# Turning adj in blocks of 512 rows by 128 columns, out of place

## What is computed

```python
# layer 0: attention with 4 heads, adj as bias and as mask
scores = einsum('hnd,hmd->hnm', qh, kh) * SCALE + graph_bias * adj
scores = where(adj == 0, -1e9, scores);  out = softmax(scores) @ vh ...  @ Wout + bout
# layer 1: graph attention, mask adj > 0 or diagonal
h = softmax(where(mask, leaky_relu(e_src[:, None] + e_dst[None, :]), NEG_INF)) @ (x @ W)
# layers 2 and 3: with d = adj.sum(axis=1) ** -0.5
h = (d[:, None] * adj * d[None, :]) @ x @ W        # then + b, or relu
# after each: x = layernorm(x + h)
```

## Time and profile before

| | us |
|---|---|
| median of 3 runs | 3061.91 |
| lowest and highest | 3058.38, 3064.88 |
| the profiled execution | 3062.02 |
| its span | 3060.1 |

### The profile page before, as it was taken

One profiled execution on the slowest core, in us unless ns is written; L12 is line 12 of the kernel. 1 busy time (PEld: TensorE's weight loads), 2 busy tenths in 40 slices (PEclk: granted clock), 3 DMA queues, 4 the chain that ended last, 5 costly groups with the idle time before them and its releaser, 6 DMA issues.

```text
span 3060.1 us, 45164 instructions
## 1 busy us (share of the span) xinstructions
PE 2959.7 (97%) x16612; PEld 2186.8 (71%) x16612; DVE 2104.1 (69%) x3607; ACT 1885.9 (62%) x2705; POOL 756.0 (25%) x454
## 2 busy tenths in 40 slices
PE   8999999999999999999998899999999999999998
PEld 5677777777777777777776555555558888788887
DVE  6677777777777777777766977777636545565464
ACT  4677777777777777777775677777653333433332
POOL 2123311333113321233210355555501001000000
PEclk9999999999999999999999999999999999999999
DMA  5699998899989998999947243333079988989882
GB/s 184 137 181 193 186 191 175 187 192 207 169 186 190 187 205 178 179 192 195 197 100 278 88 145 137 124 138 138 21 178 212 217 199 201 218 204 218 203 196 59
DMA packets 707435, 534.41 MB, mean 175 GB/s; under 512 B 563728, under 2 KB 603920, under 8 KB 690832
## 3 DMA queue, kind: packets, MB, share of 16 engines
q1 hardware_dynamic: 682176, 445.00, 65.1%
q10 hardware_dynamic: 18144, 66.07, 8.0%
q0 software_dynamic: 6896, 20.45, 2.3%
HBM read 443.29 MB, written 88.08 MB: 174 GB/s over the span
## 4 chain that ended last, share of the span: by engine, by line
PE 68%; DMA 11%; DVE 7%; issue 5%; SPq 4%; POOL 3%; ACT 2%; POOLq 0%; DVEq 0%; ACTq 0%
PE gl_four L1475 12%; PE at_o L606 9%; PE gl_quad L1528 7%; PE gl_quad L1529 7%; PE gl_quad L1530 7%; PE at_turn L580 6%; PE at_turn L593 5%; DMA adjT<-at_probs 4%; PE at_score L580 3%; PE gl_quad L1458 3%; DMA at_probs<-in_adj 3%; PE at_score L593 3%; SPq L404 3%; DMA at_bias<-in_adj 2%; POOL at_masked L503 2%
## 5 line engine op out<-in xcount | busy, mean ns | idle before, releaser
L717 ACT ACTIVATE at_probs<-at_probs,at_minus_max 128x1024 f32<-128x1024 f32 x512 | 581.6, 1139 | 9.6 <-DVE at_minus_max L871 8.7
L866 DVE CUSTOM_DVE_ANT_0 at_probs<-at_turn,at_bias 128x1024 f32<-128x1024 f32 x336 | 407.1, 1212 | 172.4 <-PE at_turn L580 167.3
L503 POOL TENSOR_SCALAR at_masked<-at_bias 128x512 bf16<-128x512 f32 x180 | 365.6, 2043 | 630.9 <-DMA at_bias<-in_adj 624.7
L726 ACT ACTIVATE at_pT<-at_turn 128x1024 f32<-128x1024 f32 x342 | 346.0, 1024 | 252.2 <-PE at_turn L593 251.9
L606 PE MATMUL at_o<-at_pT,at_values 128*64 128x256 f32 x4096 | 470.3, 382 | 0.0
L1475 PE MATMUL gl_four<-gl_early,gl_first_wh 128*128 128x512 f32 x1024 | 460.8, 593 | 6.0 <-ACT gl_early L1596 6.0
L1621 ACT ACTIVATE gl_split<-gl_units 128x1024 fp32r<-128x1024 f32 x256 | 263.7, 1055 | 278.6 <-PE gl_quad L1530 278.6
L580 PE MATMUL at_turn<-at_kT,at_q 128*128 128x512 f32 x1344 | 397.7, 418 | 22.6 <-DVE at_maxima L866 22.6
L1528 PE MATMUL gl_quad<-gl_split,gl_rows_hi 128*128 128x512 f32 x1024 | 403.0, 394 | 6.0 <-DVE gl_split L1809 6.0
L606 PEld LDWEIGHTS at_o<-at_pT,at_values 128*64 128x64 f32 x4096 | 282.5, 137 | 172.8 <-issue 43.2
L1529 PE MATMUL gl_quad<-gl_split,gl_rows_hi 128*128 128x512 f32 x1024 | 399.2, 390 | 0.0
(11 more groups left out here) (135 smaller groups left out, 3880.6 us busy)
## 6 DMA issues: line engine op xcount, KB each, us to landing
gl_units<-adjT SPq DMA_DIRECT2D x512, 256.0 KB, 7.9
at_bias<-in_adj SPq DMA_DIRECT2D x128, 512.0 KB, 6.1
at_probs<-in_adj SPq DMA_DIRECT2D x256, 256.0 KB, 5.4
adjT<-at_probs SPq DMA_DIRECT2D x1024, 64.0 KB, 4.9
gl_first_weights<-in_adj SPq DMA_DIRECT2D x32, 2048.0 KB, 8.2
at_values<-v_heads ACTq DMA_DIRECT2D x126, 512.0 KB, 5.6
gl_early<-x SPq DMA_DIRECT2D x160, 128.0 KB, 2.7
x<-gl_early POOLq DMA_DIRECT2D x64, 128.0 KB, 2.7
```

The costliest lines, as they stand in the source:

```text
L503: pool.tensor_scalar(masked[:, g % MASKS, :], part, 0.0, MASKED / SCALE, ALU.is_equal, ALU.mult)\
L717: act.activation(part, part, ACT.Exp, bias=minus_max[:, k, t:t + 1], scale=1.0, accum_out=sums[:, k, t, pp:pp + 1]).then_inc(prob_ready, 1)
L726: act.activation(pT[:, j % PT_SLOTS, :], place[:], ACT.Copy).then_inc(pT_ready, 1)
L866: dve.tensor_tensor_reduce(out=ring[:, place_in_ring(u, pp), t, :], in0=place[:], in1=bias[:, t, at], scale=SCALE, scalar=LOWEST, op0=ALU. ...
```

## The change

A block becomes 512 rows x 128 columns, four tiles of 128 rows side by side in a partition. It is loaded in runs of 512 bytes. VectorE writes the turned squares to a second buffer, with the four tiles of one square column side by side, so that a run of the store is 4 x 32 words, 512 bytes. Of the four places two are now for loaded and two for turned blocks. SyncE waits for the turn of block b, then issues the load of b+2, then the four stores of b. VectorE waits, before it turns block b, also for the stores of b-2. In `adjT` the 512 rows of a set now stand in the order (group of 32, tile, row in the group) instead of (tile, group, row), and `keep_out` puts them back in order when it copies the results of layers 2 and 3. The number of blocks, their beats, the number of DMAs and the bytes stay.

```diff
-    BLOCK = 4 * P
+    SET = 4 * P
     BLOCK_TILES = 4
-    BLOCK_SETS = N // BLOCK
-    BLOCKS = NT * BLOCK_SETS
+    BLOCK = BLOCK_TILES * P
+    ROW_BLOCKS = N // P
+    BLOCKS = NT // BLOCK_TILES * ROW_BLOCKS
+    BLOCK_KEYS = P // SQUARE
...
-        squares = probs[:, 0:BLOCK_PLACES * BLOCK].rearrange("p (b n) -> p b n", b=BLOCK_PLACES)
+        squares = probs[:, 0:2 * BLOCK].rearrange("p (b t n) -> p b t n", b=2, t=BLOCK_TILES)
+        turned_squares = probs[:, 2 * BLOCK:4 * BLOCK].rearrange("p (b k t i) -> p b k t i", b=2, k=BLOCK_KEYS, t=BLOCK_TILES)
...
             def load_block(b):
-                row_tile, n = block_at(b)
-                sync.dma_start(squares[:, b % BLOCK_PLACES, :], adj_tiles[:, row_tile, n * BLOCK:(n + 1) * BLOCK])\
-                    .then_inc(block_loaded[b % BLOCK_PLACES], 16)
+                rows, n = block_at(b)
+                sync.dma_start(squares[:, b % 2, :, :],
+                               adj_tiles[:, rows * BLOCK_TILES:(rows + 1) * BLOCK_TILES, n * P:(n + 1) * P])\
+                    .then_inc(block_loaded[b % 2], 16)
             def store_block(b):
-                row_tile, n = block_at(b)
-                sync.wait_ge(block_turned, b + 1)
-                to = adjT.rearrange("j (s k r) -> j s k r", k=BLOCK_TILES * SQUARES, r=BLOCK)
+                rows, n = block_at(b)
+                to = adjT.rearrange("j (s k r) -> j s k r", k=SET // SQUARE, r=SET)
+                k = n * BLOCK_KEYS % (SET // SQUARE)
                 for g in range(SQUARES):
-                    at = row_tile % BLOCK_TILES * P + g * SQUARE
-                    sync.dma_start(to[:, row_tile // BLOCK_TILES * BLOCK_SETS + n, :, at:at + SQUARE],
-                                   squares[g * SQUARE:(g + 1) * SQUARE, b % BLOCK_PLACES, :]
-                                   .rearrange("j (k i) -> j k i", i=SQUARE))\
-                        .then_inc(block_stored[b % BLOCK_PLACES], 16)
+                    at = g * BLOCK_TILES * SQUARE
+                    sync.dma_start(to[:, rows * (N // SET) + n * P // SET, k:k + BLOCK_KEYS, at:at + BLOCK_TILES * SQUARE],
+                                   turned_squares[g * SQUARE:(g + 1) * SQUARE, b % 2, :, :, :].rearrange("j k t i -> j k (t i)"))\
+                        .then_inc(block_stored[b % 2], 16)
...
-            for b in range(3):
+            for b in range(2):
                 load_block(b)
             def store_turned(c, side, r):
                 for b in blocks_in(c, side, r):
+                    sync.wait_ge(block_turned, b + 1)
+                    if b + 2 < BLOCKS:
+                        load_block(b + 2)
                     store_block(b)
-                    if b + 3 < BLOCKS:
-                        wait(sync, block_stored[(b + 3) % BLOCK_PLACES], 16 * SQUARES * ((b + 3) // BLOCK_PLACES))
-                        load_block(b + 3)
...
             def turn_block(b):
-                dve.wait_ge(block_loaded[b % BLOCK_PLACES], 16 * (b // BLOCK_PLACES + 1))
-                part = squares[:, b % BLOCK_PLACES, :]
-                dve.transpose(part, part).then_inc(block_turned, 1)
+                dve.wait_ge(block_loaded[b % 2], 16 * (b // 2 + 1))
+                wait(dve, block_stored[b % 2], 16 * SQUARES * (b // 2))
+                dve.transpose(turned_squares[:, b % 2, :, :, :], squares[:, b % 2, :, :].rearrange("p t (k i) -> p k t i", i=SQUARE))\
+                   .then_inc(block_turned, 1)
...
-            copy(outT[:, half, :], bank).then_inc(outT_ready[half], 1)
+            if C < CHUNKS:
+                copy(outT[:, half, :], bank).then_inc(outT_ready[half], 1)
+            else:
+                copy(outT[:, half, :].rearrange("p (t g i) -> p g t i", t=CT, g=SQUARES),
+                     bank.rearrange("p (g t i) -> p g t i", t=CT, g=SQUARES)).then_inc(outT_ready[half], 1)
```

More of the change, by code:

```diff
@@ L144, in __init__ @@
         self.ident_made = space.sem("ident_made")
-        self.block_stored = [space.sem(f"block_stored{k}") for k in range(4)]
+        self.block_stored = [space.sem(f"block_stored{k}") for k in range(2)]
         self.x1_stored = x1_stored
@@ L272, in layer0_attention @@
         adj_loaded = [sp.sem(f"adj_loaded{i}") for i in range(BEATS)]
-        block_loaded = [sp.sem(f"block_loaded{k}") for k in range(BLOCK_PLACES)]
+        block_loaded = [sp.sem(f"block_loaded{k}") for k in range(2)]
         block_turned = sp.sem("block_turned")
@@ L296, in layer0_attention @@
         shared.turned_but_one = BEATS * (UNITS - 1)
-        shared.blocks_stored = [16 * SQUARES * len(range(k, BLOCKS, BLOCK_PLACES)) for k in range(BLOCK_PLACES)]
+        shared.blocks_stored = [16 * SQUARES * len(range(k, BLOCKS, 2)) for k in range(2)]
         WEIGHT_LOADS = 2
@@ L352, in block_at @@
         def block_at(b):
-            return b // BLOCK_SETS, b % BLOCK_SETS
+            return b // ROW_BLOCKS, b % ROW_BLOCKS
         def place_of(g):
```

## The result

| kernel | median us | lowest to highest |
|---|---|---|
| before, beside it | 3060.14 | 3055.4 to 3064.88 (4 runs) |
| changed | 3029.47 | 3026.33 to 3032.35 (4 runs) |

The ratio is 0.990, with a 95% interval of 0.988 to 0.992: 31 us faster, 27 were forecast. On another chip the kernel before took 3089 and 3090 us in two sets of runs; there the changed kernel took 3030.9, a ratio of 0.981 (0.979 to 0.983).

A forecast was written before the change was run, and what follows sets the result against it. TensorE was taken as the bound, idle in attention through late masks behind full DMA queues. 3062 us less 31 for relieved queues plus 4.5 for two places gave 3035.5, so 3035 us, range 3016 to 3062.

The forecast's parts named there:

- What bounds the kernel: Attention: TensorE 97% busy; its 32.3 us idle mostly from late GpSimd masks, as full queues delay SyncE's bias loads.
- Part 1, the packets: Attention's block transfers: 512-byte stores at 43 ns, loads 37 ns; a block 41 us instead of 60, share 0.92 to 0.71.
- Part 2, the crowded stretch: Sides 2 to 4 of an attention chunk: overrun falls from 9.5 to 2.8 us, late masks go, 31 us won in all.
- part 3: Two places in attention: VectorE waits for stores of b-2, near 1.7 us each; cost 4.5 us, bounds 0 and 50.
- cover of 2 us: VectorE's turns in attention: a wait up to about 2 us costs TensorE nothing, from 2.04 us seen at (3,2).
- The three spots: Tight turns in each attention chunk: (2,1) to (2,3), (3,0) to (3,2), (7,0) to (7,2), store waits 0 to 3.1 us.
- Part 4: Turn in attention and reordered copy in the last two layers: turn stays 706 ns, copy adds 0 (at most 6 us).
- B: Rival, attention's three tight places: VectorE's wait for the stores of b-2 replaces the mask wait, 3103 us; chance 0.12.
- The mark of 2.7 us a wait: VectorE's waits at attention's turns: from 2.7 us each, the slower outcome was to decide.
- C: Rival, DMA queues: packets cost by bytes, a block 64 us instead of 60, masks stay late, 3060 us; chance 0.08.
- A: Rival, attention: all TensorE waits go, packets cost near the lower end (25 us a block), 3021 us; chance 0.17.
- The other signs: Whole kernel and attention: 387,264 packets, share 0.65 to 0.8, mask waits below 10 us, bias pieces issued within 5 us.

The follow-up runs named there:

- order-only run: Kernel before with only the changed order and places (two loaded, two turned; load ahead of stores), blocks and 128-byte stores unchanged: 3192.3 us, ratio 1.043.
- the run with bias loads first: Kernel before with the load of a bias piece moved ahead of the block's stores and load in SyncE's program: 3085.5 us, ratio 1.007.

## Why the prediction was right

**What bounds the kernel** held. TensorE's idle time was put down to late masks and those to SyncE's lateness. With the DMA time gone the mask waits went, and with them 29.0 us of idle came down to 13.7 us. The step needs one correction, from the order-only run and the run with bias loads first: the masks were where the lateness showed, and not a cause that could be cured by itself.

**Part 1, the packets**, was right in direction, too small in sum and wrong in one term. The forecast was 19 us of one engine less for a block and a share of 0.71; by chunk it is (1422 - 993) / 17 = 25 us and 0.64. The 128-byte store was sized right (22 to 24 ns measured, 24 used), the 512-byte store nearly (45 to 52 against 43). The load was the mis-sized term: 8 us dearer was forecast, and it came out up to 6 us cheaper. The value of 37 ns was an interpolation towards a row of 1 KB loads, and for the long run I took the rate of a stretch with large loads only; the run with short loads on the kernel before shows that 2 KB loads in this crowd cost no less for their bytes.

The rule of the Trainium skill (DMA: Bandwidth & Descriptors, Specifications) that runs of 512 bytes reach line rate is not borne out for these stores: 45 to 52 ns for 512 bytes is 10 to 11 GB/s for an engine, against 23.5 for large runs. What the Trainium skill says of a row pitch of 2 MiB in HBM (the same page, Latency and other measured facts) is measured with that pitch from partition to partition; here it lies between the four runs of one partition, and loads with such runs were not slower. The measurements decide here.

**Part 2, the crowded stretch**: a chunk with masks in time was put at 94.9 us. The fourteen took 1335.9 us, 95.4 each with their three stalls and 95.1 without them. The idle left was put at 0.52 us from the best chunk of before; it is 0.98 in each. For the stretch from 177.03 on, 26.6 less 4.5 us for part 3, that is 22.1 us, was forecast, and 22.3 measured. That these agree so closely is luck: the fourteen chunks came out 3 us longer in all than 14 x 94.9, and the 3 us allowed for a granted clock of 0.98 were not needed, as it was 1.00 in every one of them.

The sign "TensorE's idle in 177 to 1535 below 12 us" did not come true: it is 17.8 us in the like stretch, 13.7 of them the one wait a chunk that the prediction had put at 0.52 us, 7.3 in all. The 22.3 us won are 14.5 of idle time and 7.8 of busy time: TensorE is busy 1325.5 us before and 1317.8 now over the same 14 x 668 matmuls. The clock explains a part of the second, as the next lines show.

Ahead of the stretch 3.9 us were won where 4.5 were forecast. The 3.3 us won behind it had no term in the forecast. Some 1.9 us of them lie ahead of the first wait for ScalarE in the last chunk (from 1535.18 to 1616.08 before, from 1508.99 to 1588.01 now). The 25 us behind the last wait, before and now (columns as in rows 2):

```profile
1535.00:1560.00 25.00, 24.82 (x163) 19.32 (x164) 19.45 (x36) 16.11 (x24) 4.51 (x2) 0.93 0.72 122
```
```profile
1509.00:1534.00 25.00, 25.00 (x175) 19.55 (x176) 19.14 (x35) 18.20 (x28) 1.33 (x1) 1.00 0.50 136
```

In the kernel before the clock stood at its lower level, 1.2 GHz, for a few us behind the wait of 3.18 us:

```profile
1537.00:1539.00 2.00, 2.00 (x9) 1.80 (x9) 1.57 (x5) 0.69 (x1) 2.00 (x2) 0.50 0.66 120
```

Behind the wait of 0.98 us it stayed at 2.4 GHz. So a long wait cost more than its own length. By the means of the 25 us, 0.93 and 1.00, that is 1.8 us, an estimate. The other 1.4 us of the 3.3 lie behind 1616.08 and 1588.01 and were not looked into.

**Part 3, two places**: waits near 1.7 us, three to a chunk, were forecast. Measured are 51 of 1.64 us on average, 83.5 us in all, a little over the 80 that were called right. The cost was put at 4.5 us; TensorE's waits outside the regular 0.98 sum to 4.1 us from 173.11 to 1508.99. So the size was right, but the rule behind it was not. The prediction compared each wait with a cover of 2 us. VectorE's timeline shows the two places where TensorE paid most:

```profile
805.19 0.71 DVE L889 STREAM_TRANSPOSE at_probs<-at_probs 128x512 f32<-128x512 f32 x1 [2.54 <-DMA adjT<-at_probs]
...
808.34 0.71 DVE L889 STREAM_TRANSPOSE at_probs<-at_probs 128x512 f32<-128x512 f32 x1 [1.31 <-DMA adjT<-at_probs]
...
815.96 0.71 DVE L889 STREAM_TRANSPOSE at_probs<-at_probs 128x512 f32<-128x512 f32 x1 [2.62 <-DMA adjT<-at_probs]
...
1092.19 0.71 DVE L889 STREAM_TRANSPOSE at_probs<-at_probs 128x512 f32<-128x512 f32 x1 [1.25 <-DMA adjT<-at_probs]
...
1097.85 0.71 DVE L889 STREAM_TRANSPOSE at_probs<-at_probs 128x512 f32<-128x512 f32 x1 [3.83 <-DMA adjT<-at_probs]
```

Between the waits of each group VectorE never waits for TensorE, so they add up: 6.47 us cost TensorE 2.49, and 5.08 us cost 1.33. In the two traces of the changed kernel it is the same sum that counts everywhere: 3.96, 4.12, 4.14 and 4.25 us cost 0.20, 0.37, 0.38 and 0.50, and sums below 3.96 us cost no wait that the timeline shows. The kernel with stores first agrees (4.80 us cost 1.05), and so does the one with long loads (4.31 cost 0.55). The cover is thus near 3.75 us (3.98 in the group of three), counted from VectorE's last wait for TensorE and for all waits since, and not 2 us for each. The 2.04 us at (3,2) that the prediction went by had merely cost nothing.

The three spots were not right either: the regular waits stand at (3,1), (3,2) and (7,1), fifteen each; of the other six one is at (2,3). It is not the distance in time that tells them apart. VectorE comes to the turn at (3,1) 5.9 us (median) after the turn of b-2 has ended and always waits; it comes to (2,3) after 4.9 us and waited once. So the stores of the block at (2,3) land later than those of (2,1); at (3,1) loads of values and bias pieces are in the queues too, but what delays the stores there was not tested.

**Part 4** held:

```profile
L889 DVE STREAM_TRANSPOSE at_probs<-at_probs x256: 700/707/716, 100.4 to 1530.7; 128x512 f32<-128x512 f32 x128
```
```profile
L1571 DVE COPY gl_early<-gl_quad x16: 691/692/692, 2304.3 to 3015.5; 128x512 f32<-128x512 f32 x16
```

Reading in runs of 32 words out of place costs nothing (707 against 706 ns), nor does the reordered copy: 692 ns on VectorE and 598 on ScalarE, the same as before the change.

**The rivals.** B was real and large, and it was kept away by part 1 alone: without the relief it gives 3189 to 3192 us, where I had 3103. Its lateness was priced at 5.5 us landing at three spots, while there 94 and 105 waits of 2.4 and 2.0 us on average arise from 100 to 1500 us. The mark of 2.7 us a wait, from which B was to decide, would have missed it: there were twice as many waits as it counted, and waits add up. C was excluded by the share. A needed the 0.98 us to go as well, which took an edit that the change does not hold.

**The other signs.** The packets, the waits for masks (none left) and the turn's 716 ns at most came as said, and the one load of piece 5 that was looked at left 2.2 us after its release. The share of 0.64 lies just under the 0.65 to 0.8 that was given. Of the 51 waits at the turn one, of 3.83 us, is above the 2.7 that would have proved part 3 wrong.

## What to carry over

When several transfers share one queue, the consumer that waits last is where the lateness shows. Two kernels here had that wait cured by order alone, and another consumer paid more. Before you move transfers about in such a queue, work out the demand by stretch, in engine time: packets by their own price, not bytes. A change that both relieves the queue and takes away depth should be costed with each half alone; here the loss of depth alone costs 4.3%, a relief alone (half the store runs) brings 1.2%, and the change with both brings 1%.

The stretch in which another engine can hold up TensorE begins where that engine last waited for TensorE. Its delays since that point add up and cost nothing until they have used up the slack, here 3.75 us. Work taken out ahead of that point brought nothing, work taken out behind it brought the whole wait.

## What I had not expected of the hardware

- A store run of 512 bytes took 45 to 52 ns of a DMA engine, one of 128 bytes 21 to 24 ns. Four times the bytes for twice the time.
- Loads of 512-byte runs kept the engines busy no longer than 2 KB runs of the same bytes (by chunk 1337 against 1422 us on the kernel before, 993 against 1007 on the changed one).
- What SyncE issues right behind four stores takes longer when the stores are of 2048 short runs. A block's load in that place: 1.23 us (median) in the kernel before, 0.45 with half the store runs and 0.45 in the changed kernel with stores first. Ahead of the stores it takes 0.43 us even in the order-only kernel.
- Behind a wait of TensorE of 3.18 us the granted clock was at its lower level (0.50 from 1537 to 1539 us) and 0.93 over 25 us; behind one of 0.98 us it stayed at 1.00.
- The kernel before took 3060 to 3064 us (medians) on the other chips and 3089 to 3090 us on one; the changed one took 3029.5 and 3030.9 us on the two chips where it ran.
